# Two heads at once on the two row halves of TensorE: float32r scores in 50 rows, and the masks of the maxima on VectorE

## The chip, the cores and the metric

The kernel runs on one core of a Trainium2 chip. The metric is the device time of one execution in microseconds (us). Engines are called as in the profile: PE is TensorE (PEld its weight loads), DVE is VectorE, ACT is ScalarE, POOL is GpSimd, SP is the engine whose queue issues nearly all transfers.

## What is computed

The reference is a chain of two transformer layers on 4096 tokens of width 256 with 16 heads of 16. What matters here are three attentions. The first (sparse) gives each query its own block of 128 keys and every eighth key of the whole sequence, with a causal mask of -10000 on both; the two others (dense) are causal over all 4096 keys.

```
w = jnp.einsum('bhnqd,bhnkd->bhnqk', fq, fk) * scale + fmask
w = jax.nn.softmax(w, axis=-1)
o1 = jnp.einsum('bhnqk,bhnkd->bhnqd', w, fv).reshape(B, Hn, L, d)
```

Around them stand the projections (among them an 8-bit product), norms, rotary positions and a layer of four experts.

## The kernel before

The program has five stages: embedding (norm, query-key-value projection, 8-bit product), the sparse attention, a middle stage (projections, norms, rotary positions), the two dense attentions as one stage, and the experts. All order is written out by hand; engines meet at semaphores alone.

For scores a float32 query or key is cut into three bf16 parts (`p1`, `p2`, `p3` in the embedding, `parts` in the middle stage; the second part is made by ACT, the third by POOL). `TERMS` lists six products of such parts, so a head's score is one bf16 matmul with 6 x 16 = 96 rows of contraction. Three more rows (`MROWS`) carry the negated maximum of the query against ones in the keys: 99 rows.

The attention function `attend` works in units: one unit is one strip of 512 queries (j) of one group of 4 heads. Its keys come in chunks of 128 (dense: 4(j+1) chunks; sparse: 4 chunks of strided keys and one of the queries' own blocks, called local). Four kinds of work stand in one list, `order`, which every engine walks in the same order:

- "tile": scores of 128 queries against up to 512 keys, for the maxima (L692 dense, L681 and L688 sparse), with its mask added by a matmul with an identity (L695, L683, L685). DVE reduces the tile to a maximum (L805, L795 to L801). Tiles, and two rarer things, the turned maxima ("hand") and the turned output ("out"), share three PSUM banks in turn: item e waits until item e-3 was read.
- "negate": the maximum over a unit's tiles, negated and cut in three bf16 parts by DVE (L818 to L824); PE turns it (L700), DVE copies it (L830), and a transfer (L641) puts it in the queries' last rows.
- "score": scores of 128 keys against 512 queries for one head (L718, L725, L733), on the diagonal with a mask by matmul (L721, L728, L730). ACT takes the exponential of two heads at once (L776).
- "weigh": the values weighed by the exponentials (L756), the four heads of a group in four column quarters of the array, one chunk behind the scores.

Tiles run ahead of the scores by up to 36 chunks (`lead`); one tile is put behind each score, so a chunk in the steady state is score, tile, score, tile, score, tile, score, tile, weigh. Units lengthen in one group (4, 8, ... 32 chunks) and shorten in the next.

## Time and profile before

| | us |
|---|---|
| median of 3 runs (5483.14 to 5489.94) | 5484.69 |
| the profiled execution: its time | 5488.33 |
| its span | 5486.5 |
| embedding, 0 to 251 | 251 |
| sparse attention, 251 to 955 | 704 |
| middle, 955 to 1378 | 423 |
| dense attentions, 1378 to 4731 | 3353 |
| experts, 4731 to 5486 | 755 |
| PE busy | 4990.8 (91%) |
| DVE busy | 4167.8 (76%) |
| ACT busy | 2924.5 (53%) |

The span is the time from the first to the last record of the trace; the execution's own time is 1.8 us longer. Matmul records overlap in time, since they are pipelined and their ends are modelled: what one costs is read from start to start, not from its length. The busy share of PE is for this reason near the top where the array is merely kept supplied.

### The profile page before, as it was taken

Reading aid. Unit: us, or ns where it says so; the run is one execution under the profiler, and the core shown is the slowest. Engines: PE = TensorE matmul, PEld = TensorE weight load, DVE = VectorE, ACT = ScalarE, POOL = GpSimd, SP = SyncE. Lnnn points to the kernel's source line nnn. Section 1 sums busy time; section 2 is a strip of 40 time slices with the busy share of each in tenths; the row PEclk is TensorE's granted clock in tenths of the full one; section 3 lists DMA queues with packets and bytes.
Section 4 is the critical chain, followed back from the end, with each engine's and each line's share of the span. In section 5 each row is a group of like instructions: output and inputs, shape, how many; then the busy total and the mean of one; then the engine's idle time right before and its main releaser. Section 6 shows DMA issues by size and latency. Waiting matters only on the chain.

```text
span 5486.5 us, 80549 instructions
## 1 busy us (share of the span) xinstructions
PE 4990.8 (91%) x32000; PEld 2370.9 (43%) x32000; DVE 4167.8 (76%) x8394; ACT 2924.5 (53%) x3357; POOL 341.4 (6%) x308
## 2 busy tenths in 40 slices
PE   5378999665699999999999999999999999899999
PEld 4333444554233333433333333333333333488888
DVE  7566777576688888888888888888888877455555
ACT  3334555333255666666666666666666666432322
POOL 2210000355000000000000000000000000200000
PEclk8779999887799999999999999999999999899999
DMA  3554321354600120210210310200300000201010
GB/s 119 135 94 68 50 47 23 125 168 151 98 15 11 19 39 15 33 36 9 26 26 15 44 26 9 45 7 19 58 11 6 9 9 9 68 20 39 20 39 9
DMA packets 268673, 242.18 MB, mean 44 GB/s; under 512 B 73212, under 2 KB 247804, under 8 KB 264060
## 3 DMA queue, kind: packets, MB, share of 16 engines
q1 hardware_dynamic: 268296, 237.02, 19.5%
q8 instruction: 253, 4.15, 0.3%
q14 instruction: 124, 1.02, 0.1%
HBM read 143.49 MB, written 92.27 MB: 43 GB/s over the span
## 4 chain that ended last, share of the span: by engine, by line
PE 82%; DVE 9%; SPq 3%; ACT 2%; issue 2%; DMA 1%; POOL 0%; ACTq 0%; POOLq 0%; DVEq 0%
PE psum L756 21%; PE psum L718 19%; PE psum L692 17%; PE psum L73 12%; DVE maxes_dense L805 2%; PE psum L725 2%; PE psum L681 2%; SPq L607 2%; PE psum L721 1%; PE psum L695 1%; PE psum L704 1%; PE psum L1508 1%; SPq L593 1%; DMA keys_sparse<-parts_scratch 1%; PE psum L730 1%
## 5 line engine op out<-in xcount | busy, mean ns | idle before, releaser
L805 DVE TENSOR_REDUCE maxes_dense<-psum 128x1 f32<-128x512 f32 (+3 forms) x4608 | 2706.8, 640 | 508.6 <-PE psum L692 295.8
L776 ACT ACTIVATE probs_dense<-psum 128x1024 f32<-128x1024 f32 (+3 forms) x2304 | 2100.4, 951 | 1106.4 <-PE psum L718 819.8
L692 PE MATMUL psum<-keys_dense,queries_dense 96*128 96x512 bf16 (+3 forms) x4608 | 1693.8, 369 | 68.2 <-DMA queries_dense<-parts_scratch 55.6
L718 PE MATMUL psum<-queries_dense,keys_dense 99*128 99x512 bf16 (+3 forms) x4608 | 1669.6, 367 | 8.3 <-ACT probs_dense L776 7.2
L756 PE MATMUL psum<-probs_dense,values_dense 128*32 128x512 f32 (+3 forms) x9216 | 1133.4, 569 | 0.0
L718 PEld LDWEIGHTS psum<-queries_dense,keys_dense 99*128 99x128 bf16 x4608 | 447.5, 98 | 1164.4 <-ACT probs_dense L776 878.4
L692 PEld LDWEIGHTS psum<-keys_dense,queries_dense 96*128 96x128 bf16 x4608 | 451.6, 98 | 532.0 <-DVE maxes_dense L805 260.5
L795 DVE TENSOR_REDUCE maxes_sparse<-psum 128x1 f32<-128x144 f32 (+23 forms) x512 | 217.4, 425 | 189.5 <-PE psum L683 186.8
L1615 ACT ACTIVATE activated<-psum 128x512 f32<-128x512 f32 x208 | 124.6, 599 | 417.7 <-PE psum L73 406.3
L776 ACT ACTIVATE probs_sparse<-psum 128x1024 f32<-128x1024 f32 x224 | 226.7, 1024 | 217.0 <-PE psum L728 80.4
L756 PEld LDWEIGHTS psum<-probs_dense,values_dense 128*32 128x32 f32 x9216 | 187.9, 108 | 349.4 <-issue 300.3
L725 PE MATMUL psum<-queries_sparse,str_keys 99*128 99x512 bf16 x512 | 196.8, 388 | 71.2 <-DMA queries_sparse<-neg_rows_sparse 70.1
L681 PE MATMUL psum<-str_keys,queries_sparse 96*128 96x512 bf16 x512 | 203.8, 399 | 59.2 <-POOL str_keys L854 55.6
L695 PE MATMUL psum<-tri_query,ident_bf 128*128 128x128 bf16 x1024 | 227.1, 222 | 0.0
L721 PE MATMUL psum<-tri_key,ident_bf 128*128 128x128 bf16 x1024 | 224.9, 221 | 0.0
L1750 DVE CAST hid_high<-activated 128x512 fp32r<-128x512 f32 x208 | 95.6, 460 | 144.2 <-ACT activated L1615 141.5
L797 DVE TENSOR_REDUCE maxes_sparse<-psum 128x1 f32<-128x496 f32 (+9 forms) x496 | 204.8, 413 | 0.0
L1794 POOL CAST e_down_high<-stage 128x192 fp32r<-128x192 f32 (+1 forms) x10 | 3.5, 354 | 2764.0 <-DMA stage<-in_L_ffn_e_down 2764.0
L1752 DVE TENSOR_TENSOR hid_low<-activated,hid_high 128x512 fp32r<-128x512 f32 x208 | 146.4, 704 | 7.2
L756 PE MATMUL psum<-probs_sparse,str_values 128*32 128x512 f32 x1024 | 136.4, 605 | 0.0
L695 PEld LDWEIGHTS psum<-tri_query,ident_bf 128*128 128x128 bf16 x1024 | 101.3, 99 | 78.9
L776 ACT ACTIVATE probs_sparse<-psum,after_bias 128x1024 f32<-128x1024 f32 x96 | 103.5, 1113 | 56.4 <-PE psum L725 56.4
(298 smaller groups left out, 5621.6 us busy)
## 6 DMA issues: line engine op xcount, KB each, us to landing
parts_scratch<-part SPq DMA_DIRECT2D x72, 512.0 KB, 4.1
v_scratch<-ve_s SPq DMA_DIRECT2D x96, 256.0 KB, 2.8
queries_dense<-parts_scratch SPq DMA_DIRECT2D x384, 64.0 KB
keys_dense<-parts_scratch SPq DMA_DIRECT2D x42, 512.0 KB, 16.9
keys_sparse<-parts_scratch SPq DMA_DIRECT2D x24, 512.0 KB, 18.9
queries_sparse<-parts_scratch SPq DMA_DIRECT2D x192, 64.0 KB
ao_scratch<-aos_dense SPq DMA_DIRECT2D x64, 128.0 KB, 2.0
ao_s<-ao_scratch SPq DMA_DIRECT2D x16, 512.0 KB, 4.6
```

Of the source, the lines that this page charges most:

```text
L73: m = pe.matmul(out_ap, left(l, c), right(r, c), start=(n == 0), stop=(n == len(pairs) - 1))
L681: pe.matmul(bank, q[0:TROWS, h, b * P:(b + 1) * P], str_keys[n // STRIPS % 2][0:TROWS, h, :], start=True, stop=False)
L692: m = pe.matmul(bank[:, 0:width], q[0:TROWS, h, b * P:(b + 1) * P], k[0:TROWS, h, kc * STRIP:kc * STRIP + width], start=True, stop=kc != j)
L695: m = pe.matmul(bank[:, b * P:(b + 1) * P], ident_bf[:], tri_query[:], start=False, stop=True)
L718: m = pe.matmul(full[:, first_col:STRIP], k[:, h, c * P:(c + 1) * P], q[:, h, first_col:STRIP], start=True, stop=not diagonal)
L721: m = pe.matmul(full[:, first_col:first_col + P], ident_bf[:], tri_key[:], start=False, stop=True)
L725: m = pe.matmul(full, str_keys[n // STRIPS % 2][:, h, c * P:(c + 1) * P], q[:, h, :], start=True, stop=not partly)
L756: m = pe.matmul(psum[own_rows, 4, cols], vt, probs[(2 * m_at + h // 2) % 6][:, h % 2, cols], start=(c == 0), stop=(c == sizes[n] - 1 and b ...
L776: act.activation(probs[i % 6][:, :, first_col:STRIP], psum[:, at2:at2 + 2, first_col:STRIP], ACT.Exp, scale=SCALE, **extra).then_inc(exp_d ...
L795: m = dve.tensor_reduce(mx[:, h * BLOCKS + b, 0:1], bank[:, 0:after], AX.X, ALU.max)
L797: m = dve.tensor_reduce(mx[:, h * BLOCKS + b, 2:3], bank[:, after:NSTR], AX.X, ALU.max)
L805: m = dve.tensor_reduce(mx[:, h * BLOCKS + b, kc:kc + 1], bank[:, 0:width], AX.X, ALU.max)
```

## The change

Queries and keys are cut in two float32r parts ("high" and "low") instead of three bf16 ones, so three products remain: 48 rows of contraction, 50 with the negated maximum's two parts. Two heads of a group lie in partitions 0 to 49 and 64 to 113 of one tensor, and their matmuls go to the upper and lower 64 rows of the array. Scores are emitted as a pair behind every second head, then two tiles. The mask of a tile on the diagonal, and that of strided tiles, no longer comes from PE: DVE adds a mask from SBUF and takes the maximum in one instruction (`tensor_tensor_reduce`). The masks of local tiles and of scores stay on PE. The third part, and the passes of ACT and POOL that made it, go.

```diff
-TERMS = ((0, 0), (0, 1), (1, 0), (1, 1), (0, 2), (2, 0))
+TERMS = ((0, 0), (0, 1), (1, 0))
 TROWS = len(TERMS) * HEAD_DIM
-MROWS = 3
+MROWS = 2
+SROWS = TROWS + MROWS
+HALF = P // 2
+PAIRS = GROUP // 2
...
-            return [(kc, h, b) for kc in range(j + 1) for h in range(GROUP) for b in range(BLOCKS)]
+            return [(kc, 2 * i + odd, b) for kc in range(j + 1) for i in range(PAIRS) for b in range(BLOCKS) for odd in range(2)]
...
-                    emit_tiles(4 * (m + lead(n)) + h + 1)
+                    if h % 2 == 1:
+                        emit_tiles(4 * (m + lead(n)) + h + 1)
...
-            keys = [sbuf(st, f"keys_{stage}_{i}", [TROWS + MROWS, GROUP, TOKENS], BF16) for i in range(2)]
+            keys = [sbuf(st, f"keys_{stage}_{i}", [P, PAIRS, TOKENS], F32R) for i in range(2)]
...
-                        sp.dma_start(queries[n % held][TROWS:TROWS + MROWS, :, :].rearrange("s h (b p) -> s (h b) p", p=P),
-                                     neg_rows[n % 2][:]).then_inc(queries_in[n % 8], 16)
+                        for odd in range(2):
+                            first_row, rows = odd * HALF + TROWS, MROWS * PAIRS * BLOCKS
+                            sp.dma_start(queries[n % held][first_row:first_row + MROWS, :, :].bitcast(F32).rearrange("s h (b p) -> s (h b) p", p=P),
+                                         neg_rows[n % 2][odd * rows:(odd + 1) * rows, :].bitcast(F32)).then_inc(queries_in[n % 8], 16)
...
+                            add_masks([bank], ident_h, tri0_q, True, False)
+                            for i in range(PAIRS):
+                                for block in (b, b + 1):
+                                    own, col = j * STRIP + block * P, (2 * i + block - b) * P
+                                    m = pe.matmul(bank[:, col:col + P], q[rows(h, TROWS), i, block * P:(block + 1) * P],
+                                                  k[rows(h, TROWS), i, own:own + P], start=False, stop=(i == PAIRS - 1 and block > b))
...
-                            m = pe.matmul(bank[:, 0:width], q[0:TROWS, h, b * P:(b + 1) * P],
-                                          k[0:TROWS, h, kc * STRIP:kc * STRIP + width], start=True, stop=kc != j)
-                            if kc == j:
-                                m = pe.matmul(bank[:, b * P:(b + 1) * P], ident_bf[:], tri_query[:], start=False, stop=True)
+                            m = pe.matmul(bank[:, 0:width], q[rows(h, TROWS), h // 2, b * P:(b + 1) * P],
+                                          k[rows(h, TROWS), h // 2, kc * STRIP:kc * STRIP + width], start=True, stop=True)
...
+                            for odd, full in enumerate(pair):
+                                own = rows(odd, SROWS)
+                                m = pe.matmul(full[:, first_col:STRIP], k[own, h // 2, c * P:(c + 1) * P], q[own, h // 2, first_col:STRIP],
+                                              start=True, stop=not diagonal)
                             if diagonal:
-                                m = pe.matmul(full[:, first_col:first_col + P], ident_bf[:], tri_key[:], start=False, stop=True)
+                                m = add_masks([full[:, first_col:first_col + P] for full in pair], ident_bf, tri_key, False, True)
...
+                            if e >= 2:
+                                dve.wait_ge(side_freed, e - 1)
+                            m = dve.tensor_tensor_reduce(out=masked_scores[e % 2][:, 0:width], in0=bank[:, 0:width], in1=mask, scale=1.0, scalar=-3e38,
+                                                         op0=ALU.add, op1=ALU.max,
+                                                         accum_out=mx[:, h * BLOCKS + b, 0:1] if sparse else mx[:, h * BLOCKS + b, kc:kc + 1])
...
-                for half in range(2):
-                    act.wait_ge(rested, 2 * s + half + 1)
-                    act.activation(p2[:, fs, :], rest[:, fs, :], ACT.Copy).then_inc(p2_set, 1)
```

PE in the dense stage of before, in a chunk with full scores and diagonal tiles and the start of the next (L718 is the score, L692 the tile, L695 its mask, L756 the weighing):

```order
L718 MATMUL psum<-queries_dense,keys_dense 128x512
L692 MATMUL psum<-keys_dense,queries_dense 128x128
L695 MATMUL psum<-tri_query,ident_bf 128x128
L718 MATMUL psum<-queries_dense,keys_dense 128x512
L692 MATMUL psum<-keys_dense,queries_dense 128x256
L695 MATMUL psum<-tri_query,ident_bf 128x128
L718 MATMUL psum<-queries_dense,keys_dense 128x512
L692 MATMUL psum<-keys_dense,queries_dense 128x384
L695 MATMUL psum<-tri_query,ident_bf 128x128
L718 MATMUL psum<-queries_dense,keys_dense 128x512
L692 MATMUL psum<-keys_dense,queries_dense 128x512
L695 MATMUL psum<-tri_query,ident_bf 128x128
```

The same kind of place in the changed program (L740 is the score, L712 the tile, L781 the weighing; x2 is two heads):

```order
L781 MATMUL psum<-probs_dense,values_dense 32x512 x4
L740 MATMUL psum<-queries_dense,keys_dense 128x512 x2
L712 MATMUL psum<-keys_dense,queries_dense 128x128 x2
L740 MATMUL psum<-queries_dense,keys_dense 128x512 x2
L712 MATMUL psum<-keys_dense,queries_dense 128x256 x2
L781 MATMUL psum<-probs_dense,values_dense 32x512 x4
```

The tiles' masks have left PE, and a chunk has two narrow or two wide pairs of tiles, not one of each width. Now PE where scores are on the diagonal and tiles full, changed program (L678 is the mask of the scores, on the whole array):

```order
L781 MATMUL psum<-probs_dense,values_dense 32x512 x4
L740 MATMUL psum<-queries_dense,keys_dense 128x256 x2
L678 MATMUL psum<-tri_key,ident_bf 128x128 x2
L712 MATMUL psum<-keys_dense,queries_dense 128x512 x2
L740 MATMUL psum<-queries_dense,keys_dense 128x256 x2
L678 MATMUL psum<-tri_key,ident_bf 128x128 x2
L712 MATMUL psum<-keys_dense,queries_dense 128x512 x2
L781 MATMUL psum<-probs_dense,values_dense 32x384 x4
```

Before, each of the four scores had its own mask behind it and then its tile; now the masks of two heads stand between the pair of scores and the pair of tiles. In the sparse stage, PE at the local tiles, changed program (L678 the mask, L708 four matmuls of 128 columns of one tile, L749 the scores):

```order
L749 MATMUL psum<-queries_sparse,str_keys 128x512 x2
L678 MATMUL psum<-tri_q,ident_h 128x512
L708 MATMUL psum<-keys_sparse,queries_sparse 128x128 x4
L678 MATMUL psum<-tri_q,ident_h 128x512
L708 MATMUL psum<-keys_sparse,queries_sparse 128x128 x4
```

Before, mask and four matmuls (L685, L688) were on the whole array and one score stood ahead of each such tile; now the masks are on the whole array and the four matmuls on one half of it.

## Rows read from the trace of the kernel before

**Rows 1.** Windows, us: PE, PEld, DVE, ACT, POOL busy (count), granted clock, DMA, GB/s.

```profile
251.00:955.00 704.00, 590.41 (x4974) 267.29 (x4974) 492.51 (x1424) 334.95 (x338) 27.79 (x16) 0.90 0.35 59
...
1378.00:4731.00 3353.00, 3291.95 (x20800) 1143.12 (x20800) 2800.86 (x5120) 2139.43 (x2369) 15.76 (x20) 0.98 0.14 24
```

**Rows 2.** Timeline of a full dense chunk: start us, length us, engine, instruction, idle before.

```profile
2590.15 1.06 PE L756 MATMUL psum<-probs_dense,values_dense 128*32 128x512 f32 x8
...
2591.15 0.39 PE L718 MATMUL psum<-queries_dense,keys_dense 99*128 99x512 bf16 x1
...
2591.37 0.38 PE L692 MATMUL psum<-keys_dense,queries_dense 96*128 96x512 bf16 x1
...
2591.79 2.48 DVE L805 TENSOR_REDUCE maxes_dense<-psum 128x1 f32<-128x512 f32 x4 [0.36 <-PE psum L692]
...
2592.54 0.10 PEld L692 LDWEIGHTS psum<-keys_dense,queries_dense 96*128 96x128 bf16 x1 [0.19 <-DVE maxes_dense L805]
2592.68 0.38 PE L692 MATMUL psum<-keys_dense,queries_dense 96*128 96x512 bf16 x1
...
2592.99 1.06 PE L756 MATMUL psum<-probs_dense,values_dense 128*32 128x512 f32 x8
```

**Rows 3.** Timeline of PE at diagonal chunks of the dense stage.

```profile
2188.85 1.06 PE L756 MATMUL psum<-probs_dense,values_dense 128*32 128x512 f32 x8
...
2191.41 0.22 PE L721 MATMUL psum<-tri_key,ident_bf 128*128 128x128 bf16 x1
2191.47 0.38 PE L692 MATMUL psum<-keys_dense,queries_dense 96*128 96x512 bf16 x1
...
2199.32 0.86 PE L756 MATMUL psum<-probs_dense,values_dense 128*32 128x256 f32 x16
...
2207.30 1.07 PE L756 MATMUL psum<-probs_dense,values_dense 128*32 128x512 f32 x8
...
2210.06 1.07 PE L756 MATMUL psum<-probs_dense,values_dense 128*32 128x512 f32 x8
```

**Rows 4.** Timeline of PE at float32r matmuls of the middle and expert stages.

```profile
1092.28 0.50 PE L73 MATMUL psum<-w_rotary_high,xt_high 128*128 128x512 f32 x1 [0.38 <-DVE rot L1261]
1092.62 0.39 PE L73 MATMUL psum<-w_rotary_low,xt_high 128*128 128x512 f32 x1
1092.84 0.40 PE L73 MATMUL psum<-w_rotary_high,xt_low 128*128 128x512 f32 x1
...
4941.79 0.25 PE L73 MATMUL psum<-gate_w_high,xft_low 128*128 128x4 f32 x1
4941.91 0.25 PE L73 MATMUL psum<-gate_w_high,xft_high 128*128 128x4 f32 x1
```

**Rows 5.** Timeline of DVE in the expert stage: tensor_tensor_reduce at 256 columns.

```profile
4745.47 0.42 DVE L1647 CUSTOM_DVE_ANT_0 junk<-xa_s 128x256 f32<-128x256 f32 x1
...
4745.94 0.43 DVE L1647 CUSTOM_DVE_ANT_0 junk<-xa_s 128x256 f32<-128x256 f32 x1
```

**Rows 6.** Sparse stage: timeline of PE, then the chain's two weighings a unit apart.

```profile
415.32 0.38 PE L685 MATMUL psum<-tri_q,ident_h 128*128 128x512 f16 x1
...
415.76 0.38 PE L725 MATMUL psum<-queries_sparse,str_keys 99*128 99x512 bf16 x1
...
425.79 1.97 PE psum L756 x40
...
444.71 1.97 PE psum L756 x40
```

**Rows 7.** The chain that ended last, embedding and middle: start us, us, what.

```profile
98.49 0.94 ACT part L316
...
233.43 4.39 POOL part L463 x2
...
1312.79 2.15 POOL part L1331
```

**Rows 8.** Window of a stretch with tiles alone; columns as in rows 1.

```profile
1448.00:1452.00 4.00, 4.00 (x8) 0.67 (x7) 4.00 (x8) 0.00 (x0) 0.00 (x0) 0.50 1.09 123
```

More of the change, by code:

```diff
@@ L457, in embed_pool @@
             for s in range(STRIPS):
-                for half in range(2):
-                    fs = slice(2 * half, 2 * half + 2)
-                    pool.wait_ge(p2_set, 2 * s + half + 1)
-                    if half == 0 and s >= 1:
-                        pool.wait_ge(parts_stored, 48 * s)
-                    pool.tensor_tensor(p3[:, fs, :], rest[:, fs, :], p2[:, fs, :], ALU.subtract).then_inc(p3_set, 1)
                 if s + 1 < STRIPS:
@@ L575, in attend @@
             masks = []
+            masked_scores = [sbuf(st, f"masked_scores_{stage}_{i}", [P, STRIP]) for i in range(2)]
+            if not sparse:
+                causal_add = sbuf(st, "causal_add", [P, STRIP], BF16)
             if sparse:
-                str_keys = [sbuf(st, f"str_keys_{i}", [TROWS + MROWS, GROUP, NSTR], BF16) for i in range(2)]
+                after_add = sbuf(st, "after_add", [P, 2 * NSTR - P // STRIDE], F16)
+                str_keys = [sbuf(st, f"str_keys_{i}", [P, PAIRS, NSTR], F32R) for i in range(2)]
                 str_values = [sbuf(st, f"str_values_{i}", [P, NSTR // P, GROUP * GCOL]) for i in range(2)]
@@ L619, in attend_sp @@
                 for tile in keys:
-                    sp.dma_start(tile[TROWS:TROWS + MROWS, :, :], d["c_ones"]).then_inc(masks_in, 16)
+                    for odd in range(2):
+                        first_row = odd * HALF + TROWS
+                        sp.dma_start(tile[first_row:first_row + MROWS, :, :].bitcast(F32), ones_d).then_inc(masks_in, 16)
                 if sparse:
@@ L659, in attend_pe, with rows, add_masks @@
             def attend_pe():
-                pe.wait_ge(masks_in, 16 * (len(masks) + 2))
+                def rows(h, n):
+                    return slice(h % 2 * HALF, h % 2 * HALF + n)
+                def add_masks(banks, eye, mask, start, stop):
+                    for bank in banks:
+                        m = pe.matmul(bank, eye[:], mask[:], start=start, stop=stop)
+                    return m
+                pe.wait_ge(masks_in, 16 * (len(masks) + 4))
                 for kind, n, what in order:
@@ L681, in attend_pe @@
-                            pe.matmul(bank, q[0:TROWS, h, b * P:(b + 1) * P], str_keys[n // STRIPS % 2][0:TROWS, h, :],
-                                      start=True, stop=False)
-                            m = pe.matmul(bank[:, own:own + P // STRIDE], ident_h[:], mask_q[:], start=False, stop=True)
+                            m = pe.matmul(bank, q[rows(h, TROWS), h // 2, b * P:(b + 1) * P], str_keys[n // STRIPS % 2][rows(h, TROWS), h // 2, :],
+                                          start=True, stop=True)
@@ L684, in attend_pe @@
                         elif kc == "local":
-                            pe.matmul(bank, ident_h[:], tri0_q[:], start=True, stop=False)
-                            for h in range(GROUP):
-                                own = j * STRIP + b * P
-                                m = pe.matmul(bank[:, h * P:(h + 1) * P], q[0:TROWS, h, b * P:(b + 1) * P],
-                                              k[0:TROWS, h, own:own + P], start=False, stop=(h == GROUP - 1))
+                            add_masks([bank], ident_h, tri0_q, True, False)
@@ L850, in compact @@
                         pool.wait_ge(first_keys_in, 96)
-                        pool.wait_ge(masks_in, 16 * (len(masks) + 2))
+                        pool.wait_ge(masks_in, 16 * (len(masks) + 4))
                     if group >= 1:
                         pool.wait_ge(keys_in[group % 2], 96 * (group // 2 + group % 2))
-                    pool.tensor_copy(str_keys[group % 2][:], keys[group % 2][:, :, STRIDE - 1::STRIDE]).then_inc(compacted, 1)
+                        pool.wait_ge(compacted, 2 * group)
+                    if group == 2:
+                        pool.wait_ge(split_done, len(chunks))
+                    for odd in range(2):
+                        own = slice(odd * HALF, odd * HALF + SROWS)
+                        pool.tensor_copy(str_keys[group % 2][own, :, :], keys[group % 2][own, :, STRIDE - 1::STRIDE]).then_inc(compacted, 1)
                 if sparse:
```

222 lines of the change are left out of this document (110 added, 112 removed).

## The prediction

> **What bounds the kernel now.** I read the busy time by stage first [rows 1]: the dense stage is 3353 of 5486.5 us, with PE busy 3292 and DVE 2801 of them; the sparse stage is 704, PE 590. A faster PE looks like the whole answer. The timeline of one steady chunk [rows 2] says how much of it can be had. A chunk is four scores (S, L718), four tiles for the maxima (T, L692) and the weighing (V, L756); V starts at 2590.15 and again at 2592.99, so it takes 2.84 us. PE: eight matmuls of 0.22, 0.09 more before V, and 1.00 from V to the next S. DVE: four reductions, 2.48, then 0.36 idle.
>
> The reader is to see a ring in those rows. T goes round three banks, so the fourth T of a chunk needs the bank of its first. DVE starts that first tile at 2591.79; the weight load of the fourth T starts at 2592.54 (0.75 on), its matmul at 2592.68, V at 2592.99 (0.31), the next S 1.00 later (2590.15 to 2591.15), the next T 0.22 later, and DVE takes it up 0.42 after its start. 0.75 + 0.14 + 0.31 + 1.00 + 0.22 + 0.42 = 2.84: already as long as PE's own work. Only the 0.14, in which that matmul waits for an array still at work, goes with a faster PE. So no full chunk can come below 0.75 + 0.31 + 1.00 + 0.22 + 0.42 = 2.70, whatever two heads at once save: the 3-bank ring is what decides.
>
> **The change, part by part.** The sum is made against the profiled execution's 5488.3 us (span 5486.5), 3.6 above the median of the runs.
>
> *Dense, full chunks.* Four S and four T become two pairs each, in the order S pair, T pair, S pair, T pair, V. The ring stays: the fourth T still waits for the first one's bank, and V and an S pair still stand between it and the next T. New in it is the weight load of a float32r operand. Rows at 2.4 GHz show it [rows 4]: with 4 columns a matmul still takes 0.11 to 0.12 after another, so the load sets a floor of 0.11; and the first matmul after a wait is followed 0.34 later (1092.28 to 1092.62) where the one after takes 0.22, so a load that nothing hides costs some 0.11. With bf16 S follows V, and T a wait, with no such cost [rows 2]. In the ring the load is bare twice: at the fourth T, whose load holds the wait, and at the first S after V. A pair, if its halves overlap, takes two loads one after the other, 0.22, about the 0.22 of its columns: so the T after it starts as late as now. The ring is then 0.75 + 0.11 + 0.31 + 1.00 + 0.11 + 0.22 + 0.43 = 2.93, that is 0.09 longer. PE's own work falls to about 2.1, so PE idles where it now works.
>
> *Chunks on the diagonal.* Units have 4, 8, ... 32, 32, ... 4 chunks and the last four of each are diagonal; tiles run 36 chunks ahead, so of 1152 chunks 736 are full in both streams, 160 have only S diagonal, 160 only T, 96 both. Both: 2188.85 to 2199.32 is four chunks, 2.62 each [rows 3]; only T: 2207.30 to 2210.06, 2.76. Only S: 2.62 + four T wider by 0.02, 2.70. The masks of S stay on PE, on the whole array (0.06 each, 2191.41 to 2191.47), between pairs on halves. V's 0.09 is the price of one change between forms of the array that I have. A diagonal S in the ring then costs 0.11 load, 0.11 second load, 0.13 mean columns, 0.09 change, 0.12 two masks, 0.09 change, 0.11 load: 0.76 for 0.33. With V narrower (0.90 as a mean of the four, by its columns) the ring is 0.75 + 0.11 + 0.31 + 0.90 + 0.76 + 0.43 = 3.26, or +0.56. With T diagonal too, the maxima are the new add-and-max with masks: at 256 columns 0.47 from one to the next [rows 5], so some 0.34 to 0.74 for 128 to 512; the ring's first tile is then 128 or 384 wide, and I get 2.96, +0.34. Only T diagonal: T's masks leave PE, the ring has a short first tile in one of two chunks: 2.66, -0.10. Its extra 0.14 of DVE a tile against a reduction hides in the same idle time of DVE; uncovered it would be 1024 x 0.14 = 143 us.
>
> *Once a unit.* Negation loses two of five DVE steps of about 0.2 that now hold the next reductions; the hand-over becomes two transfers, on a queue that waits for DVE anyway. I take -0.3 x 64 = -20 us.
>
> Dense: 736 x 0.09 = 66, 160 x 0.56 = 90, 96 x 0.34 = 33, 160 x -0.10 = -16, units -20: **+150 us**. The ends: bare loads and changes at nothing, full chunks 2.70, T-diagonal ones about 2.45, S-diagonal as now: -103 - 48 - 16 - 20 = -187. Halves that don't overlap: full chunks 3.17 (+0.24 for the pair in the ring), S-diagonal ones some 0.8 to 1.0 longer, in all about +480.
>
> *Sparse.* A unit takes 18.9 us (425.79 to 444.71) [rows 6], mostly PE's. A local tile is now 0.44 (415.32 to 415.76). It becomes a mask 0.22, change 0.09, four float32r matmuls of 128 columns on one half, 0.11 bare and four times 0.11, change 0.09: 0.95. Four are +2.0; the S pairs there give 0.4 back. A local score pair is two masks 0.44, 0.20 and 0.09 for two changes with a bare load, and eight loads 0.88: 1.61, two of them 3.2 where 1.8 stood, less 0.5 for the T pairs: +0.8. A strided tile is one add-and-max of 512, about 0.73, for two reductions that together read as much; in the one chunk without V, which DVE bounds, I take +0.3 for four; two chunks on the ring +0.1 each, negation -0.4. +2.5 x 32 = **+80 us**; with loads of two halves side by side and free changes about -30, at twice these prices +190.
>
> *Embedding and middle.* The third part and its two passes go. The chain has ACT L316 0.94 in each of eight strips and POOL 4.39 at the end [rows 7]; the middle has L1331 2.15 and its like at its last strips, some 11 us as an estimate. What it writes grows by a third; these stores are waited for only at a stage's end. **-25 us** (-40 to -10); the first keys' 33 us load keeps its bytes.
>
> Sum: 5488 + 150 + 80 - 25 = 5693, by the median 5690. I say **5685**.
>
> On the price of a change the Trainium skill is firmer than my one row. "TensorEngine Tiling (Array Packing)", Key Properties, says that changing the tiling mode, not just the tile, drains TensorE. V's 0.09 agrees, and at nothing per change the sum would be near 5600. "TensorE: Matmul & The Clock Gate", Part 3, has packed tiles start about 4 ns apart and loads overlap only with matmuls on other row groups. The float32r rows disagree with the second: full-array matmuls stand 0.22 apart with a load of their own between them. By it the next T's load would come after the S pair, 0.11 more a chunk, near 5800.
>
> **The rivals.** *Faster.* Loads bare in my count are hidden, by V's own tail or by the other half, and changes cost little: the ring drops to 2.70 and masks leave PE for good. For: bf16 rows show nothing bare, and DVE would stay under it at 2.41. Against: [rows 4]. All of it gives 5488 - 187 - 30 - 25 = 5246; it decides from about half my prices down, where the three terms cancel.
>
> *Halves don't overlap.* For: no row here has two row halves. Against: V's four heads on column quarters do run together, four passes of 512 columns for each head in 1.00. It gives 5488 + 480 + 130 - 25, about 6070.
>
> *The clock falls.* The full chunk streams 1.8 us of columns in 2.93, 61%, where it was 92%. For: at 1448 to 1452, with tiles alone, eight in 4 us, the granted clock is 0.50, that is 1.2 GHz [rows 8]. Against: that stretch streams 36%. One chunk in ten at 1.2 GHz, each some 1.9 us longer, is +220: 5900.
>
> **How the numbers follow.** Forecast, 5560 to 5830: 0.50. Faster, 5250 to 5470: 0.25. No overlap: 0.10. Clock: 0.10. Near no change, all small prices: 0.05. The range 5400 to 5930 leaves out the deep half of the faster case and of the no-overlap case. A measurement tells 0.2% from no change: faster 0.25, same 0.05, slower 0.70.
>
> **What would show it.** After the change a full chunk's V should come every 2.9 us, with PE idle before the fourth T for half a microsecond and DVE idle 0.4 to 0.5 before the first; L740's two records within 0.12; diagonal chunks over 3.0; sparse units 21 us; embedding and middle 25 us shorter; granted clock 0.98 as now. I am wrong if V comes every 2.75 or less (loads hidden), if diagonal chunks stay at 2.7 (changes free), or if L740 records stand 0.23 apart (no overlap).

## The result: 7.0% slower

| | us |
|---|---|
| before, median of 4 runs (5483.14 to 5492.96) | 5487.31 |
| changed, median of 4 runs (5843.5 to 5890.69) | 5878.3 |
| ratio, 95% interval | 1.0702, 1.0653 to 1.075 |
| profiled execution of the changed kernel, its span | 5890.69, 5888.9 |
| its PE, DVE, ACT busy | 5226.1 (89%), 4067.5 (69%), 2863.9 (49%) |
| its mean granted clock (before) | 0.883 (0.945) |

The direction and the outer range of the prediction (5400 to 5930) held; the time is 193 us above the 5685 forecast and outside the 5560 to 5830 that had a chance of 0.50. It lies by the 5900 of the clock rival, which had 0.10. First the busy tenths of PE and the granted clock in 40 slices of the changed kernel's span:

```profile
PE   5488989776599999999999999999999999899999
PEclk8676877877568999998999979999999999999999
```

The clock falls in the sparse stage (slices 3 to 8) and at places of the dense one that had 0.98 before [rows 1]. To place the loss I cut both traces at the weighings V: the windows of the kernel before from its first V to its last in the sparse and in the dense stage, columns as in rows 1:

```profile
316.00:973.00 657.00, 583.88 (x5043) 266.09 (x5045) 470.01 (x1358) 345.95 (x349) 24.02 (x15) 0.95 0.30 52
1435.00:4726.00 3291.00, 3266.61 (x20703) 1133.51 (x20701) 2776.33 (x5067) 2135.31 (x2365) 15.37 (x18) 0.99 0.13 23
```

The same two windows of the changed kernel:

```profile
295.00:1113.00 818.00, 738.30 (x4553) 335.39 (x4556) 435.51 (x1276) 343.58 (x348) 24.86 (x18) 0.79 0.23 42
1566.00:5129.00 3563.00, 3336.08 (x19697) 1332.31 (x19700) 2734.88 (x5936) 2120.65 (x2364) 15.41 (x18) 0.92 0.11 21
```

From the start to the first V: 316 to 295, -21. Sparse: 657 to 818, +161. To the first dense V: 462 to 453, -9. Dense: 3291 to 3563, +272. Behind it: -1. Sum +402, the difference of the spans.

How much of it is clock? The trace's clock records put 542 us of that dense window at 1.2 GHz (61 before) and 345 us of the sparse one (72 before). I compared each chunk that has some time at 1.2 GHz with the median of its own kind wholly at 2.4 GHz: the dense stage loses 176 us that way (2 before). A full chunk takes 2.94 at 2.4 GHz and 4.59 at 1.2, so a us at the low clock costs 0.36, and 542 x 0.36 = 195 for 61 x 0.36 = 22 before: 173 more, which fits the 174. In the sparse stage the 28 units without a key load take 24.37 on average, the seven of them wholly at 2.4 GHz 20.52: 28 x 3.85 = 108. So **282 us of the 402 are clock, and 120 the rest**: dense +98, sparse +53, the others -31.

The full chunk is as forecast, down to the steps. Its timeline in the dense stage of the changed kernel, to be held against rows 2:

```profile
2622.14 1.06 PE L781 MATMUL psum<-probs_dense,values_dense 128*32 128x512 f32 x8
...
2623.14 0.49 PE L740 MATMUL psum<-queries_dense,keys_dense 50*128 50x512 f32 x2
2623.24 0.19 PEld L712 LDWEIGHTS psum<-keys_dense,queries_dense 48*128 48x128 f32 x2
2623.47 0.40 PE L712 MATMUL psum<-keys_dense,queries_dense 48*128 48x512 f32 x2
...
2623.71 0.40 PE L740 MATMUL psum<-queries_dense,keys_dense 50*128 50x512 f32 x2
...
2623.91 2.48 DVE L844 TENSOR_REDUCE maxes_dense<-psum 128x1 f32<-128x512 f32 x4 [0.45 <-PE psum L712]
2623.95 0.40 PE L712 MATMUL psum<-keys_dense,queries_dense 48*128 48x512 f32 x1
2624.65 0.18 PEld L712 LDWEIGHTS psum<-keys_dense,queries_dense 48*128 48x128 f32 x1 [0.75 <-DVE maxes_dense L844]
...
2625.07 1.06 PE L781 MATMUL psum<-probs_dense,values_dense 128*32 128x512 f32 x8
```

V comes every 2.93. DVE starts the first tile at 2623.91; the load of the fourth starts 0.74 on, V 0.42 behind it, the next S pair 1.00 later. The S pair after V takes 0.33, one load more than the 0.24 of every pair after it: two matmuls of 0.21 now take the time of one. The loads of the T pair start 0.10 behind the S pair, while S streams on the same two halves (2623.24): the 0.11 that would have made the sum 5800 did not appear. PE has nothing to stream from about 2624.2 to 2624.65, and DVE is idle for 0.45 ahead of the first tile.

Then a chunk where only the scores are on the diagonal (V to V 3.34, as the first of its four has the widest scores):

```profile
2263.27 1.06 PE L781 MATMUL psum<-probs_dense,values_dense 128*32 128x512 f32 x8
...
2264.27 0.49 PE L740 MATMUL psum<-queries_dense,keys_dense 50*128 50x512 f32 x2
...
2264.70 0.28 PE L678 MATMUL psum<-tri_key,ident_bf 128*128 128x128 bf16 x2
...
2264.91 0.50 PE L712 MATMUL psum<-keys_dense,queries_dense 48*128 48x512 f32 x2
...
2265.45 2.48 DVE L844 TENSOR_REDUCE maxes_dense<-psum 128x1 f32<-128x512 f32 x4 [0.85 <-PE psum L712]
...
2266.61 1.06 PE L781 MATMUL psum<-probs_dense,values_dense 128*32 128x512 f32 x8
```

Pair to masks is 0.43 where pair to tiles is 0.33, and two masks of 0.06 with the way back take 0.21: about 0.1 for each change between halves and whole array. (The operands change from f32 to bf16 there too; V behind a tile, f32 on both sides, costs the same: 0.31 after the 0.21 of the tile.) The Trainium skill, "TensorEngine Tiling (Array Packing)", Key Properties, has such a change drain the array; the trace agrees in that each one costs something, 0.09 to 0.10.

In the sparse stage, PE of the changed kernel in a unit at full clock, a local tile and the local scores:

```profile
670.26 0.39 PE L678 MATMUL psum<-tri_q,ident_h 128*128 128x512 f16 x1
670.58 0.66 PE L708 MATMUL psum<-keys_sparse,queries_sparse 48*128 48x128 f32 x4
671.17 1.06 PE L781 MATMUL psum<-probs_sparse,str_values 128*32 128x512 f32 x8
...
675.11 0.60 PE L678 MATMUL psum<-tri_k,ident_h 128*128 128x512 f16 x2
675.64 0.66 PE L759 MATMUL psum<-queries_sparse,keys_sparse 50*128 50x128 f32 x8
676.14 0.44 PE L701 MATMUL psum<-str_keys,queries_sparse 48*128 48x512 f32 x2
```

A local tile takes 0.91 (forecast 0.95). A pair of local scores takes 1.03 (forecast 1.61): its eight matmuls of 128 columns take 0.50, since their weight loads go in pairs too.

### The profile page after: what moved, and what is told of

It reads as the page before. It is cut to its first block, busy times and chain, and to the rows that moved or that the text cites. A ratio compares the mean times of both kernels' runs of the same rounds, so it can differ in the third digit from the quotient of the medians.

```text
span 5888.9 us, 79808 instructions
## 1 busy us (share of the span) xinstructions
PE 5226.1 (89%) x30464; PEld 2657.0 (45%) x30464; DVE 4067.5 (69%) x9211; ACT 2863.9 (49%) x3309; POOL 242.7 (4%) x265
## 4 chain that ended last, share of the span: by engine, by line
PE 71%; DVE 16%; issue 5%; SPq 3%; ACT 3%; DMA 2%; POOL 0%; DVEq 0%; ACTq 0%; POOLq 0%
PE psum L781 21%; PE psum L712 16%; PE psum L76 12%; PE psum L740 10%; DVE maxes_dense L844 9%; PE psum L678 4%; PE psum L701 2%; SPq L614 2%; PE psum L708 1%; PE psum L749 1%; ACT probs_dense L801 1%; DMA queries_sparse<-neg_rows_sparse 1%; PE psum L722 1%; PE psum L1531 1%; SPq L598 1%
## 5 line engine op out<-in xcount | busy, mean ns | idle before, releaser
L844 DVE TENSOR_REDUCE maxes_dense<-psum 128x1 f32<-128x512 f32 x3584 | 2226.8, 684 | 553.4 <-PE psum L712 552.9
L712 PE MATMUL psum<-keys_dense,queries_dense 48*128 48x512 f32 (+3 forms) x4608 | 1570.1, 454 | 267.8 <-DVE maxes_dense L844 180.1
L781 PE MATMUL psum<-probs_dense,values_dense 128*32 128x512 f32 (+3 forms) x9216 | 1219.9, 608 | 0.0
L740 PE MATMUL psum<-queries_dense,keys_dense 50*128 50x512 f32 (+3 forms) x4608 | 1078.5, 457 | 11.2 <-ACT probs_dense L801 10.7
L712 PEld LDWEIGHTS psum<-keys_dense,queries_dense 48*128 48x128 f32 x4608 | 695.3, 199 | 861.2 <-DVE maxes_dense L844 626.7
L740 PEld LDWEIGHTS psum<-queries_dense,keys_dense 50*128 50x128 f32 x4608 | 469.6, 197 | 1003.6 <-ACT probs_dense L801 699.2
L837 DVE CUSTOM_DVE_ANT_0 masked_scores_dense<-psum,causal_add 128x128 f32<-128x128 f32 (+3 forms) x1024 | 448.6, 488 | 248.7 <-PE psum L712 247.5
L837 DVE CUSTOM_DVE_ANT_0 masked_scores_sparse<-psum,after_add 128x512 f32<-128x512 f32 x512 | 326.0, 688 | 250.8 <-PE psum L701 250.0
L781 PEld LDWEIGHTS psum<-probs_dense,values_dense 128*32 128x32 f32 x9216 | 192.5, 111 | 280.3 <-issue 219.2
L701 PE MATMUL psum<-str_keys,queries_sparse 48*128 48x512 f32 x512 | 196.2, 531 | 74.7 <-POOL str_keys L894 58.8
L749 PE MATMUL psum<-queries_sparse,str_keys 50*128 50x512 f32 x512 | 170.9, 542 | 64.8 <-DMA queries_sparse<-neg_rows_sparse 63.7
L841 DVE TENSOR_REDUCE maxes_sparse<-psum 128x4 f32<-128x512 f32 x128 | 88.7, 693 | 136.7 <-PE psum L708 136.7
L781 PE MATMUL psum<-probs_sparse,str_values 128*32 128x512 f32 x1024 | 175.5, 765 | 0.0
L701 PEld LDWEIGHTS psum<-str_keys,queries_sparse 48*128 48x128 f32 x512 | 83.3, 216 | 161.3 <-DVE maxes_sparse L837 81.3
L678 PE MATMUL psum<-tri_key,ident_bf 128*128 128x128 bf16 x1024 | 150.3, 230 | 0.0
L749 PEld LDWEIGHTS psum<-queries_sparse,str_keys 50*128 50x128 f32 x512 | 68.9, 223 | 160.7 <-issue 82.1
```

Source lines behind the costliest of these rows:

```text
L678: m = pe.matmul(bank, eye[:], mask[:], start=start, stop=stop)
L701: m = pe.matmul(bank, q[rows(h, TROWS), h // 2, b * P:(b + 1) * P], str_keys[n // STRIPS % 2][rows(h, TROWS), h // 2, :], start=True, stop ...
L712: m = pe.matmul(bank[:, 0:width], q[rows(h, TROWS), h // 2, b * P:(b + 1) * P], k[rows(h, TROWS), h // 2, kc * STRIP:kc * STRIP + width], ...
L740: m = pe.matmul(full[:, first_col:STRIP], k[own, h // 2, c * P:(c + 1) * P], q[own, h // 2, first_col:STRIP], start=True, stop=not diagonal)
L749: m = pe.matmul(full, str_keys[n // STRIPS % 2][own, h // 2, c * P:(c + 1) * P], q[own, h // 2, :], start=True, stop=not partly)
L781: m = pe.matmul(psum[own_rows, 4, cols], vt, probs[(2 * m_at + h // 2) % 6][:, h % 2, cols], start=(c == 0), stop=(c == sizes[n] - 1 and b ...
```

## The experiments

Two theories stood. **Ring and prices**: the loss is that of the 3-bank ring and the mode changes, and the clock only accompanies it. **Clock**: most of the loss comes from time at 1.2 GHz, which the changed kernel brings about. A third question is what part of the change could pay by itself. All edits are to the changed kernel unless another is named. The times at 1.2 GHz are those of each run's one profiled execution.

### e1_repeat: the third tile three times

```diff
+                again = 2
...
-                            m = pe.matmul(bank[:, 0:width], q[rows(h, TROWS), h // 2, b * P:(b + 1) * P],
-                                          k[rows(h, TROWS), h // 2, kc * STRIP:kc * STRIP + width], start=True, stop=True)
+                            for _ in range(1 + again * (h % 2 == 0 and b % 2 == 1)):
+                                m = pe.matmul(bank[:, 0:width], q[rows(h, TROWS), h // 2, b * P:(b + 1) * P],
+                                              k[rows(h, TROWS), h // 2, kc * STRIP:kc * STRIP + width], start=True, stop=True)
```

The strided tiles get the same loop.

> The changed kernel, with the matmul of the third tile of each chunk issued three times instead of once into its own bank (dense tiles and strided tiles; two repeats, 0.44 us of streaming in the 0.75 us in which PE waits for the bank of the fourth). Nothing else changes. Theory clock: of the 402 us that the changed kernel lost, about 310 are time at 1.2 GHz that the kernel before did not have (542 us of the dense stage and 383 of the sparse one stand at that level, 61 and 106 before), and it falls because PE streams too little. Then the repeats cost nothing in the ring (full dense chunk at full clock stays at 2.93) and give back at least a third of it: 5600 to 5780 us, granted clock 0.91 or more. Theory prices: the loss is that of the ring and of mode changes, and the clock only accompanies it. Then 5870 to 5950, clock 0.88.

Measured: 5859.99 (5826.39 to 5884.28), 1.0677 of before, 1.0626 to 1.0727. Full chunks at full clock 2.94. Time at 1.2 GHz in the two windows fell from 887 to 563 us, worth 117 at 0.36, but together they are only 61 us shorter (4320 for 4381). Part of the gain is eaten: a full chunk at 1.2 GHz is now 4.72 long for 4.59, a diagonal one 5.54 for 4.99, and at full clock chunks with both streams diagonal take 2.95 on the mean for 2.81. So repeats hold the clock up without a cost in the full chunk's ring, and this form of them costs elsewhere. The total lies between the two expectations, 10 us from that of the prices, and does not decide.

### e2_late_tile: one tile behind V

```diff
-                        emit_tiles(4 * (m + lead(n)) + h + 1)
+                        emit_tiles(4 * (m + lead(n)) + (2 if h == 1 else 3))
                 if c >= 1:
                     order.append(("weigh", n, (m - 1, c - 1)))
+                emit_tiles(4 * (m + lead(n)) + 4)
```

> The changed kernel, with one tile of each chunk emitted behind the weighing instead of ahead of it: S pair, T pair, S pair, T, V, T. Theory ring of three banks: between the reading of one tile and the start of the tile three places on, only V is left, no longer V and the S pair: 0.13 + 0.11 + 0.31 + 1.00 + 0.11 + 0.43 + 0.62 = 2.71 for a full dense chunk instead of 2.93. 736 x 0.22 = 160, some 50 at diagonal chunks, and less time at 1.2 GHz as PE idles less: 5550 to 5690 us. Theory that the ring is not what decides (DVE's latency behind each tile, or PE's own order): the full chunk stays at 2.85 to 2.95 and the time within 30 us of 5880.

Measured: 5637.63 (5631.97 to 5644.26), ratio 1.0274, 1.0257 to 1.0291: 240 us less than the changed kernel, and within the 5550 to 5690 expected. The timeline of a full chunk:

```profile
3040.99 1.06 PE L782 MATMUL psum<-probs_dense,values_dense 128*32 128x512 f32 x8
...
3041.99 0.49 PE L713 MATMUL psum<-keys_dense,queries_dense 48*128 48x512 f32 x1
...
3042.52 2.48 DVE L845 TENSOR_REDUCE maxes_dense<-psum 128x1 f32<-128x512 f32 x4 [0.21 <-PE psum L713]
...
3043.26 0.18 PEld L713 LDWEIGHTS psum<-keys_dense,queries_dense 48*128 48x128 f32 x1 [0.52 <-DVE maxes_dense L845]
...
3043.68 1.06 PE L782 MATMUL psum<-probs_dense,values_dense 128*32 128x512 f32 x8
```

2.69 from V to V (forecast 2.71), and DVE's idle time has halved, 0.45 to 0.21. The ring is shown: an edit of the order alone, with the same instructions, shortens the full chunk by what the ring says. Of the 240 us some 67 are clock: 391 and 309 us stand at 1.2 GHz for 542 and 345, and 187 x 0.36 = 67.

### e3_same_half: both tiles of a pair on one half

```diff
-for i in range(PAIRS) for b in range(BLOCKS) for odd in range(2)]
+for i in range(PAIRS) for odd in range(2) for b in range(BLOCKS)]
```

> The changed kernel, with the tiles of a pair on the same row half (two blocks of queries of one head) instead of on both: only the score pairs overlap. Theory ring: a tile pair then takes 0.44 instead of 0.24, but no tile pair stands between V and the first tile, so a full dense chunk stays at 2.93 to 2.97 at full clock; and as PE works 0.4 us more in each chunk, less time stands at 1.2 GHz: 5650 to 5880 us in all. Theory that the overlap of tiles is needed: 0.4 more a chunk, 3.3, and 6250 or more.

Measured: 6554.22 in the profiled execution, 6687.58 to 6726.6 in the three others, whose granted clock was lower still (0.739 to 0.745 for 0.767). The first expectation missed the time; the second named such a time, but not for its reason. 348 full chunks wholly at full clock take 2.94, so the ring was right and the tiles' overlap is worth nothing there. But 2146 us of the dense window stand at 1.2 GHz:

```profile
1610.00:5793.00 4183.00, 4130.53 (x19700) 1774.70 (x19699) 2779.43 (x5934) 2159.64 (x2364) 15.47 (x18) 0.74 0.09 18
```

PE is busy for 99% of it, more than in the changed kernel (94%), at a granted clock of 0.74 for 0.92. The low clock itself fills gaps, but it is not that alone: counted in full chunks wholly at full clock, PE is busy for 97% in this run and for 89% in the changed kernel. The same matmuls, laid out otherwise over the two halves, cost some 820 us of clock in this stage.

### e4_no_score_masks: dense diagonal without masks

```diff
-                                              start=True, stop=not diagonal)
-                            if diagonal:
-                                m = add_masks([full[:, first_col:first_col + P] for full in pair], ident_bf, tri_key, False, True)
+                                              start=True, stop=True)
...
-                    chain.then(dve.tensor_copy(causal_add[:, STRIP - P:STRIP], tri_query[:]))
+                    chain.then(dve.memset(causal_add[:, STRIP - P:STRIP], 0.0))
```

> The changed kernel without the causal masks in the dense stage: PE's mask matmuls on diagonal scores are left out, and the mask that DVE adds to diagonal tiles is zero (same instructions). Theory prices of mode changes: chunks with only S diagonal, 3.23 at full clock in the changed kernel, fall to 0.75 + 0.11 + 0.31 + 0.90 + 0.35 + 0.43 = 2.85; those with both from 2.78 to some 2.6; full ones stay at 2.94. At full clock -80 us in all, to about 5800. Theory that these chunks are long for another reason (narrower scores, ACT): they stay above 3.1.

Measured: one execution, 5899.79; this kernel leaves out the dense masks. At full clock, chunks with only S diagonal fell from 3.23 to 2.82 at their median (forecast 2.85), by 0.39 on the mean, those with both from 2.78 to 2.42 (forecast 2.6). So a ring with masks and mode changes in it is 0.4 longer than one without, which is what the prices give for S-diagonal chunks; for those with both I had expected only 0.2. The total did not fall, where about 5800 was expected: 853 us of its dense window stand at 1.2 GHz for 542, and take back what the masks had cost (some 110 at 0.36). Two V of a full chunk there at 1.2 GHz, 4.59 apart:

```profile
2248.49 1.93 PE L779 MATMUL psum<-probs_dense,values_dense 128*32 128x512 f32 x8
...
2253.08 1.93 PE L779 MATMUL psum<-probs_dense,values_dense 128*32 128x512 f32 x8
```

### e5_repeat_upper: the mirror image of e1_repeat

The pairs' tiles in the order `for odd in (1, 0)`, and the repeats for `h % 2 == 1`.

> The mirror image of the first run (e1_repeat): in each tile pair the head on the upper half comes first, so the third tile of a chunk, which is issued three times, lies on rows 64 to 111 and not on rows 0 to 47. PE streams for exactly as long as in e1_repeat. There the time at 1.2 GHz fell from 542 to 353 us in the dense stage and from 345 to 210 in the sparse one (first to last weighing), and full chunks at full clock stayed at 2.94. Theory A, the clock follows how long PE streams at all: same as e1_repeat, 300 to 400 and 180 to 250 us at 1.2 GHz, 5830 to 5890 in all. Theory B, it follows what the lower row half does: then the tiles of e3_same_half, all of one head in a chunk and so all on the upper half in every second chunk, are what let it fall there (2146 us), and here nothing is gained over the changed kernel: 500 us or more in the dense stage, 5880 to 5980 in all. Theory C, both halves together: in between.

Measured: 5862.25 (5844.68 to 5865.04), ratio 1.0673, 1.0657 to 1.069; 441 and 200 us at 1.2 GHz. The total is that of e1, in the range of theory A. Theory B (the lower half is what counts) falls: it does not matter which half gets more to stream. In the dense stage a repeat on the upper half helped less (441 for 353), which one profile each can't tell from scatter. Theory A (the clock follows how long PE streams at all) is taken up by e11.

### e6_late_repeat_pair and e7_late_repeat_even: repeats in the better order

Both start from e2_late_tile; the second score pair of a chunk is issued again, once as a pair (e6) or twice its lower half alone (e7):

```diff
-                            for odd, full in enumerate(pair):
-                                own = rows(odd, SROWS)
+                            for odd in (0, 1) + ((0, 1) if h == 3 and not diagonal else ()):
+                                own, full = rows(odd, SROWS), pair[odd]
```

> e2_late_tile (one tile of each chunk behind V; full chunk 2.70, 391 + 309 us at 1.2 GHz, 5638) with the second score pair of a chunk issued twice where it has no mask: 0.24 us more of both halves, in the 0.45 in which PE idles before the third tile. Theory clock: full chunks at full clock stay at 2.70 to 2.73, time at 1.2 GHz falls by a third or more (700 to below 470), each us of it costing some 0.35: 5500 to 5600. Theory that repeats only cost (what e1_repeat gave back in clock it paid in longer chunks at 1.2 GHz): 5620 to 5680.

> e2_late_tile with the lower one of the second score pair issued three times, on the lower half only: 0.44 us more of streaming on rows 0 to 49, none on the upper half. Full chunks at full clock 2.70 to 2.80. If the clock follows the lower half (theory B), time at 1.2 GHz falls below that of e6_late_repeat_pair, to 300 or less: 5470 to 5580. If it follows both halves together (theory C), the two are alike. If repeats don't hold the clock, 5640 to 5720.

Measured: e6 5579.99 (5560.69 to 5597.69), ratio 1.0165, 1.0139 to 1.0191; e7 5658.13 (5620.62 to 5716.65), 1.0288 to 1.0399 of before. Full chunks at full clock stay at 2.70 in both. e6: 251 + 219 us at 1.2 GHz where e2 had 391 + 309, and 58 us faster than e2. e7: 296 + 175 in the fastest of its four executions, and its runs lie on both sides of e2's, though its repeats stream longer. A repeat on both halves at once holds as much clock (470 and 471 us at 1.2 GHz) for half of PE's time (0.24 and 0.44 a chunk).

### e8_before_dve_masks: one part of the change on the kernel before

```diff
-                                          start=True, stop=kc != j)
-                            if kc == j:
-                                m = pe.matmul(bank[:, b * P:(b + 1) * P], ident_bf[:], tri_query[:], start=False, stop=True)
+                                          start=True, stop=True)
```

and DVE's `tensor_tensor_reduce` with its mask tiles, for dense and strided tiles, as in the change.

> The kernel before (bf16 parts in 99 rows, whole array, scores and tiles one by one) with one part of the change alone: the masks of diagonal and strided tiles added by DVE in one instruction with the maximum, their mask matmuls gone. 1024 dense masks of 0.06 and 512 sparse ones of some 0.04 leave PE, which bounds it: chunks with diagonal tiles fall from 2.76 to about 2.55 (256 of them, 50 us), sparse units by 0.6 to 1.0 us (20 to 30 us), granted clock as before. Theory of the prediction: DVE's dearer instruction hides, 5400 to 5450. Rival: DVE becomes what bounds diagonal chunks and the strided tiles, or PE's lighter load lets the clock fall: 5480 to 5560.

Measured: 5417.85 (5410.06 to 5421.54), ratio **0.9869**, 0.9854 to 0.9883: faster than both kernels, and within the 5400 to 5450 expected. Its dense window:

```profile
1414.00:4653.00 3239.00, 3209.54 (x19702) 1067.78 (x19700) 2769.03 (x6060) 2131.55 (x2364) 15.35 (x18) 0.99 0.13 23
```

3291 to 3239, at the same clock; the sparse window 657 to 642. Two V around a chunk with diagonal tiles, 2.53 apart where rows 3 have 2.76:

```profile
1681.20 1.06 PE L756 MATMUL psum<-probs_dense,values_dense 128*32 128x512 f32 x8
...
1683.73 1.06 PE L756 MATMUL psum<-probs_dense,values_dense 128*32 128x512 f32 x8
```

### e9_same_half_turns: e3 with halves in turn

```diff
-for i in range(PAIRS) for odd in range(2) for b in range(BLOCKS)]
+for i in range(PAIRS) for first in range(0, BLOCKS, 2) for odd in range(2) for b in (first, first + 1)]
```

> As e3_same_half (both tiles of a pair on one row half), but the two pairs of a chunk lie on different halves: lower, lower, then upper, upper. In e3_same_half all four tiles of a chunk were of one head and lay on one half, the next chunk's on the other; 2146 us of its dense stage stood at 1.2 GHz, at full clock its full chunks took 2.94. PE streams as long and with as many rows as there. Theory uneven halves: that one half goes short of work for a whole chunk is what let the clock fall; then here at most 600 us stand at 1.2 GHz in the dense stage, and the time is 5800 to 5950. Theory overlap: the clock falls because tiles no longer stream on both halves at once; then 1500 us or more at 1.2 GHz and 6400 to 6750. Both: full chunks at full clock stay at 2.94, as the ring does not contain the tile pair.

Measured: 6048.5 (6030.03 to 6117.8), ratio 1.1047, 1.0978 to 1.1117. Full chunks at full clock 2.93.

```profile
1598.00:5272.00 3674.00, 3459.58 (x19708) 1431.25 (x19709) 2738.03 (x5936) 2139.18 (x2364) 15.46 (x18) 0.89 0.11 20
```

779 us at 1.2 GHz, for 2146 of e3 and 542 of the changed kernel. Neither expectation's range held (5800 to 5950, 6400 to 6750); the run lies between, nearer to the first. Most of e3's fall was that one half had all tiles of a chunk; the 237 us that remain above the changed kernel go with tiles that don't stream on both halves at once.

### e10_before_masks_late: e8 with the tile behind V

The edit of e2_late_tile on e8: `emit_tiles(... + min(h + 1, 3))` at each score, `+ 4` behind the weighing.

> e8_before_dve_masks (5418; bf16 parts, whole array, masks of the maxima on DVE) with the fourth tile of each chunk emitted behind the weighing. The ring then holds V alone and no longer the score behind it, and PE's own work is what remains: 8 x 0.22 + 1.00 = 2.76 for a full chunk instead of 2.85, or 2.70 at 0.213 each. 736 x 0.09 to 0.14 = 65 to 105 us, 30 at others, granted clock as before, since PE never idles: 5290 to 5360. Rival: the last 0.09 in a chunk is PE's own (V behind a tile costs it wherever the tile stands, twice now): no gain, 5400 to 5430.

Measured: 5501.99 (5495.86 to 5507.45), ratio 1.0031, 1.002 to 1.0041: 84 us slower than e8, where 60 to 130 us faster or no change had been expected. The rival's mechanism held for full chunks, 2.85 in both:

```profile
2601.20 0.38 PE L719 MATMUL psum<-queries_dense,keys_dense 99*128 99x512 bf16 x1
...
2601.51 1.07 PE L757 MATMUL psum<-probs_dense,values_dense 128*32 128x512 f32 x8
...
2602.51 0.39 PE L695 MATMUL psum<-keys_dense,queries_dense 96*128 96x512 bf16 x1
...
2604.35 1.06 PE L757 MATMUL psum<-probs_dense,values_dense 128*32 128x512 f32 x8
```

Whatever stands ahead of V is followed by it 0.31 later, and seven matmuls of 0.22, 0.31 and 1.00 are 2.85: PE bounds this chunk, not the ring. What neither expectation had: chunks with diagonal tiles went from 2.53 to 2.66, those with both from 2.39 to 2.60 on the mean, some 37 us together, and the chunk of each unit in which the negated maxima are turned (L701) went from 3.31 to 3.94 at the median, some 40 more. In that chunk DVE does the three steps of the negation before it frees the first bank; PE then waits for DVE ahead of every tile, 0.90, 0.48, 0.49 and 0.33 at 2451 to 2453, where e8 waits 0.15 and 0.48 ahead of two. The move pays where PE idles in the ring, and costs where PE's own work fills the chunk.

### e11_repeat_pair: the second score pair three times

The edit of e6 on the changed kernel, with `(0, 1, 0, 1)`.

> The changed kernel with the second score pair of a chunk issued three times where it has no mask: PE streams for 0.46 us more a chunk, as long as the repeats of e1_repeat, but on both halves; third and fourth tile wait for it, within DVE's slack. If the clock follows how much of both halves streams, time at 1.2 GHz (542 us dense, 345 sparse in the changed kernel; 353 and 210 in e1_repeat) falls below e1_repeat's, to 250 and 150 or less; full chunks at full clock stay at 2.94. At about 0.35 us lost for each us at 1.2 GHz that gives back 150 to 200: 5690 to 5760, against some 5600 without any extra time at 1.2 GHz. If it follows only how long PE streams on any rows, it is as e1_repeat: 5830 to 5890.

Measured: 5704.71 (5700.64 to 5718.4), ratio 1.041, 1.0393 to 1.0427: **174 us less than the changed kernel, by adding work**. A full chunk, still 2.93 from V to V:

```profile
3000.98 1.06 PE L781 MATMUL psum<-probs_dense,values_dense 128*32 128x512 f32 x8
...
3002.31 0.40 PE L712 MATMUL psum<-keys_dense,queries_dense 48*128 48x512 f32 x2
3002.55 0.87 PE L740 MATMUL psum<-queries_dense,keys_dense 50*128 50x512 f32 x6
3003.26 0.72 PE L712 MATMUL psum<-keys_dense,queries_dense 48*128 48x512 f32 x2
3003.91 1.06 PE L781 MATMUL psum<-probs_dense,values_dense 128*32 128x512 f32 x8
```

and its two windows:

```profile
293.00:1038.00 745.00, 669.62 (x4948) 335.60 (x4949) 435.60 (x1274) 345.17 (x348) 24.90 (x18) 0.92 0.25 47
1491.00:4947.00 3456.00, 3431.24 (x23292) 1598.44 (x23291) 2740.82 (x5934) 2144.56 (x2364) 15.47 (x18) 0.98 0.11 22
```

165 and 124 us at 1.2 GHz for 542 and 345. The dense stage lost 107 us and the sparse one 73, with every useful instruction as it was. This settles clock against ring and prices as the cause of what I had missed. It speaks against theory A of e5 too: PE streams as long as in e1, on both halves, and 289 us stand at 1.2 GHz for 563. (The repeats stand at another place in the chunk than those of e1; e6 and e7, whose repeats stand at the same place, point the same way.)

The dense window of the runs side by side (clock and PE busy by that window's row, us at 1.2 GHz by the clock records, full chunk at full clock; for e3, the 6554.22 execution):

| | window | PE busy | clock | at 1.2 GHz | full chunk |
|---|---|---|---|---|---|
| before | 3291 | 99% | 0.99 | 61 | 2.85 |
| changed | 3563 | 94% | 0.92 | 542 | 2.94 |
| e11, scores repeated on both halves | 3456 | 99% | 0.98 | 165 | 2.93 |
| e1, tiles repeated on one half | 3543 | 99% | 0.95 | 353 | 2.94 |
| e9, tiles on one half, in turn | 3674 | 94% | 0.89 | 779 | 2.93 |
| e3, tiles on one half for a chunk | 4183 | 99% | 0.74 | 2146 | 2.94 |

## Why the prediction was right in direction and 193 us short

**The ring (right).** 2.93 forecast for a full chunk, 2.94 the median of 517 wholly at full clock; V's path, the bare loads and the idle times of PE and DVE came as written. e2 confirms it by shortening it.

**Mode changes at 0.09 (right), S-diagonal chunks (a little too dear).** The four of a unit went from 3.08, 2.87, 2.66 and 2.40 to 3.35, 3.30, 3.23 and 2.96: +0.46 on the mean where +0.56 was forecast, as I took 2.70 for 2.75 before and 3.26 for 3.21 after.

**Chunks with diagonal tiles (mis-sized).** T alone: -0.10 forecast, and 2.76 became 2.26 or 2.76 in turn, -0.25 on the mean. Both diagonal: +0.34 forecast, and 2.62 became 2.82, +0.20. The term that was wrong in both is DVE's add-and-max: I took 0.14 more than a reduction, from 256 columns in the expert stage. The changed kernel's DVE at 512 columns:

```profile
3299.66 0.69 DVE L837 CUSTOM_DVE_ANT_0 masked_scores_dense<-psum,causal_add 128x512 f32<-128x512 f32 x1
3300.27 0.08 DVE L837 DVE_READ_ACCUMULATOR2_ANT maxes_dense<- 128x1 f32 x1
```

It hands over after 0.61, a plain reduction after 0.60 (median of 3421). The sum with what was measured, 736 x 0.09 + 160 x 0.46 - 160 x 0.25 + 96 x 0.20, is 119, and with the -20 a stage for the units 99: +150 for the dense stage was +98 at full clock.

**Sparse (mis-sized).** +2.5 a unit forecast, 18.51 to 20.52 = +2.0 at full clock; the local score pair was overpriced, 1.61 for 1.03, because I let its loads go one after the other. Two such pairs make 1.2 a unit, more than the 0.5 by which the unit was off, so other terms there were too cheap; no run here tells which.

**Embedding and middle (right).** -25 forecast, -30 measured.

**The step that failed is the granted clock**: "granted clock 0.98 as now", with the clock rival at 0.10 and +220. It came true, at 282 us (174 dense, 108 sparse). The sum closes: 5693 + 282 - 52 (dense) - 27 (sparse) - 5 = 5891, the profiled execution. Two things here are luck. The miss is 193 and not some 280 only because the other terms were 84 us too dear. And the rival's +220 was worked out for full dense chunks, one in ten and 1.9 longer each; they lost some 107, at 1.65 for one wholly at 1.2 GHz, and the rest came from the other dense chunks and the sparse stage, which the rival did not have. I had the row that spoke for it, a stretch at 0.50 [rows 8], and the worked number, 61% of the chunk streamed instead of 92%; I dismissed it since that stretch streams still less, and looked only at full chunks. Those do hold the clock mostly, 517 of 587; the sparse stage and the short units don't (at 1566 to 1900, 191 of 334 us stand at 1.2 GHz), and I never worked out their share.

The rival that the halves don't overlap is out: L740's two records start 3 ns apart and a pair follows a pair by 0.24. Nor was it worth much here: e3 and e9 give up the tiles' overlap and keep 2.94.

## What to carry to other kernels

Before making a matmul cheaper, find what ring or partner engine sets the period: here halving PE's time for scores and tiles could not shorten a chunk bounded by three PSUM banks, and the thinner stream of matmuls that was left went with more time at 1.2 GHz (887 us for 133). Work out what the array still does in each stage, the short and irregular ones first, and give the clock a price of its own: with the matmuls of this chunk 0.36 us for every us at 1.2 GHz. Try a change's parts one by one: the masks on DVE alone gain 1.3%, the rest loses more than 8%; and where an engine idles inside a ring, move the long instruction so that fewer others stand between two uses of a bank (e2, -240 us; where PE's own work fills the chunk, as in e10, the same move cost 84).

## What the runs showed of the hardware

- Two float32r matmuls on the two row halves start mostly 3 or 4 ns apart (10 at most), and their weight loads go together too: eight of 128 columns take 0.50. A pair of 512 columns follows a pair after 0.24, one that follows V after 0.33.
- PE's busy share does not tell the clock: 99% busy went with 0.99, 0.98, 0.95 and 0.74 in the table above. The Trainium skill, "TensorE: Matmul & The Clock Gate", Part 1, lets the clock follow how busy PE has been; e3 disagrees if busy is what the profile's row says, also at full clock alone (97% busy in full chunks, 89% in the changed kernel). The runs order themselves by how evenly and how much both row halves stream, but none measures what is counted, and that stays open.
- Once at 1.2 GHz, e3 stayed there for up to 590 us at a time, with full chunks of 4.72.
- `tensor_tensor_reduce` at 512 columns frees DVE 0.01 us later than a plain reduction (0.61 and 0.60), so a mask added in it costs DVE next to nothing.
